# Context in two halves of tokens, the second one later, and the first norm's square root ahead of a values copy

## What is computed

```python
x = x + jnp.tanh(g_xattn[0]) * _L0_xattn_ref(_layernorm(x, axis=-1), ctx_4096, ctx_4096, pos, mask, Wq, Wk, Wv, Wo)
x = x + jnp.tanh(g_ffn[0]) * _L0_ffn_ref(_layernorm(x, axis=-1), W_q, scales, zeros, mask2, scale2, bias)
x = x + jnp.tanh(g_xattn[1]) * _L1_xattn_ref(_layernorm(x, axis=-1), ctx_4096, Wq1, bq, Wk1, bk)
x = x + jnp.tanh(g_ffn[1]) * _L1_ffn_ref(_layernorm(x, axis=-1), gate_w, expert_w, expert_b)

# in the first attention
q = (query @ Wq).reshape(nb, q_len, H, D).transpose(0, 2, 1, 3)
k = (key @ Wk).reshape(nb, q_len, KVH, D).transpose(0, 2, 1, 3)
v = (value @ Wv).reshape(nb, q_len, KVH, D).transpose(0, 2, 1, 3)
q = q * cos + _rotate_half(q) * sin
k = k * cos + _rotate_half(k) * sin
scores = jnp.where(mask == 0, -1e9, jnp.einsum("bhqd,bhkd->bhqk", q, k) / jnp.sqrt(D))
```

## Time and profile before

| what | us |
|---|---|
| median of 3 runs | 884.09 |
| lowest and highest run | 883.96 and 884.87 |
| the profiled execution's own time | 882.28 |
| its span, from the first to the last instruction | 880.5 |
| PE busy | 825.1 (94%) |
| DVE busy | 653.5 (74%) |
| POOL busy | 438.0 (50%) |
| ACT busy | 397.2 (45%) |

### The profile page before, as it was taken

One profiled execution on the slowest core, in us unless ns is written; L12 is line 12 of the kernel. 1 busy time (PEld: TensorE's weight loads), 2 busy tenths in 40 slices (PEclk: granted clock), 3 DMA queues, 4 the chain that ended last, 5 costly groups with the idle time before them and its releaser, 6 DMA issues. The chain is left out here.

```text
span 880.5 us, 13114 instructions
## 1 busy us (share of the span) xinstructions
PE 825.1 (94%) x4337; PEld 695.1 (79%) x4337; DVE 653.5 (74%) x1285; ACT 397.2 (45%) x1010; POOL 438.0 (50%) x386
## 2 busy tenths in 40 slices
PE   5889999999999999999999999999999999999980
PEld 4678888888888888888888888788778687778860
DVE  3888888867778876778876777856691658999965
ACT  4645245234334424324433433443314537879960
POOL 5489648436437634634833643530200148888840
PEclk9999999999999999999999999999999959999995
DMA  8401101101201100110220210100620677989517
GB/s 329 177 1 49 72 1 63 58 1 48 73 1 48 71 0 0 62 58 1 76 91 0 95 48 1 49 1 1 235 82 1 263 269 249 340 313 362 220 42 287
DMA packets 25945, 91.13 MB, mean 104 GB/s; under 512 B 6576, under 2 KB 7088, under 8 KB 18848
## 3 DMA queue, kind: packets, MB, share of 16 engines
q1 hardware_dynamic: 19744, 81.00, 25.1%
q0 software_dynamic: 6144, 9.46, 3.0%
HBM read 86.23 MB, written 14.68 MB: 115 GB/s over the span
## 5 line engine op out<-in xcount | busy, mean ns | idle before, releaser
L402 POOL TENSOR_TENSOR qT<-straight,turned 128x512 f32<-128x512 f32 x64 | 83.1, 1300 | 141.8 <-DVE turned L652 141.5
L518 ACT ACTIVATE probs<-bank,negmax 128x128 f32<-128x128 f32 x256 | 90.4, 365 | 130.8 <-DVE negmax L663 130.8
L652 DVE TENSOR_TENSOR turned<-bank,sinT 64x512 f32<-64x512 f32 x160 | 110.1, 688 | 2.2
L129 PE MATMUL bank<-xT_hi,wq_hi 128*128 128x512 f32 x256 | 104.2, 407 | 2.0 <-DVE xT_lo L105 2.0
L525 ACT ACTIVATE pT_hi<-bank 128x512 fp32r<-128x512 f32 x64 | 38.2, 598 | 139.0 <-PE bank L823 139.0
L131 PE MATMUL bank<-xT_hi,wq_lo 128*128 128x512 f32 x256 | 100.2, 392 | 0.0
L130 PE MATMUL bank<-xT_lo,wq_hi 128*128 128x512 f32 x256 | 100.0, 391 | 0.0
L131 PE MATMUL bank<-wo_hi,oT_lo 128*128 128x512 f32 x256 | 99.8, 390 | 0.0
L129 PE MATMUL bank<-wo_hi,oT_hi 128*128 128x512 f32 x256 | 99.7, 389 | 0.0
L130 PE MATMUL bank<-wo_lo,oT_hi 128*128 128x512 f32 x256 | 99.6, 389 | 0.0
L650 DVE TENSOR_TENSOR straight<-bank,cosT 128x512 f32<-128x512 f32 x80 | 55.3, 691 | 40.7 <-PE bank L131 36.9
(11 more groups left out here) (232 smaller groups left out, 2082.5 us busy)
## 6 DMA issues: line engine op xcount, KB each, us to landing
ring<-in_ew SPq DMA_DIRECT2D x28, 1024.0 KB, 8.8
raw_big<-in_wq SPq DMA_DIRECT2D x8, 1024.0 KB, 4.8
raw_big<-in_wo SPq DMA_DIRECT2D x8, 1024.0 KB, 4.8
early_w<-in_ew SPq DMA_DIRECT2D x8, 1024.0 KB, 10.0
ring<-picked SPq DMA_DIRECT2D x8, 512.0 KB, 7.6
raw_k<-in_wk SPq DMA_DIRECT2D x8, 256.0 KB, 5.1
ctx_raw<-in_ctxT SPq DMA_DIRECT2D x4, 512.0 KB, 6.1
raw_v<-in_wv SPq DMA_DIRECT2D x8, 256.0 KB, 5.0
```

The source lines that it names most:

```text
L129: nc.tensor.matmul(out_, hi, r_hi, start=start, stop=False)
L402: nc.gpsimd.tensor_tensor(dst, straight[:, k, :], turned[:, k, :], ALU.add).then_inc(rope_sum, 1)
L518: ex = nc.scalar.activation(probs[:, u % 2, h, :], bank_scores[u % 2][:, h * S:(h + 1) * S], ACT.Exp, bias=negmax[:, u % UNITS, h:h + 1], ...
L652: last = nc.vector.tensor_tensor(turned[dst, k, :], bank[src, :], sinT[src, tok], ALU.mult)
```

## The change

The context is fetched, copied and subtracted in two halves of tokens. The first half (tokens 0 to 511) keeps the four chunks and their places on SP, ACT and DVE, each now 128x512 in place of 128x1024. The second half is one transfer on SP behind the query weights, one ACT copy (128x2048) behind `queries_upper(0, 2)`, and one DVE subtraction (128x2048) behind `item_products(0, 2)`. It counts as the fifth step of `ctx_lo`, and PE, ACT and SP wait for five where they waited for four; on PE that wait is new and stands ahead of `make_values(0, 2)`. On ACT the square root of the first norm now stands ahead of the first values copy, with a square root of zeros before it. At the softmax of the second layer two semaphores, `g_max` and `g_nb`, became one, which counts both steps; the instructions are the same.

```diff
                     for c in range(KC):
-                        sp.dma_start(ctx_raw[:, c, :], a["ctxT"][:, c, :]).then_inc(in_ctx[c], 16)
+                        sp.dma_start(ctx_raw[:, c, 0:HALF], a["ctxT"][:, c, 0:HALF]).then_inc(in_ctx[c], 16)
...
                     sp.dma_start(raw_big[:, :], a["wq"][0].rearrange("p n -> p n")).then_inc(big_in, 16)
+                    sp.dma_start(ctx_raw[:, :, HALF:], a["ctxT"][:, :, HALF:]).then_inc(in_ctx_rest, 16)
                     sp.dma_start(mask_raw[:, :, :], a["mask"]).then_inc(in_mask, 16)
...
-                    sp.wait_ge(ctx_lo, KC)
+                    sp.wait_ge(ctx_lo, KC + 1)
                     sp.dma_start(wmask_raw[:, :, :], a["wmask"]).then_inc(f_words, 16)
...
                     for c in range(KC):
                         act.wait_ge(in_ctx[c], 16)
-                        nc.scalar.activation(cT_hi[:, c, :], ctx_raw[:, c, :], ACT.Copy).then_inc(ctx_hi, 1)
+                        nc.scalar.activation(cT_hi[:, c, 0:HALF], ctx_raw[:, c, 0:HALF], ACT.Copy).then_inc(ctx_hi, 1)
                     act.wait_ge(v_in, 32)
                     values_weight_upper(0, 0, raw_v)
                     values_weight_upper(1, 1, raw_v1)
+                    nc.scalar.activation(invtotal[:, 1, :], gates_raw[:, :], ACT.Sqrt, scale=0.0)
+                    norm_sqrt(act, 0, HALVES[0])
                     values_upper(0, 0)
-                    norm_sqrt(act, 0, HALVES[0])
                     values_upper(0, 1)
...
                     queries_upper(0, 2)
+                    act.wait_ge(in_ctx_rest, 16)
+                    nc.scalar.activation(cT_hi[:, :, HALF:], ctx_raw[:, :, HALF:], ACT.Copy).then_inc(ctx_hi, 1)
                     norm_upper(act, 0, 4)
...
-                    act.wait_ge(ctx_lo, KC)
+                    act.wait_ge(ctx_lo, KC + 1)
                     group(0, False)
...
                     for c in range(KC):
                         dve.wait_ge(ctx_hi, c + 1)
-                        nc.vector.tensor_tensor(cT_lo[:, c, :], ctx_raw[:, c, :], cT_hi[:, c, :].bitcast(F32),
+                        nc.vector.tensor_tensor(cT_lo[:, c, 0:HALF], ctx_raw[:, c, 0:HALF], cT_hi[:, c, 0:HALF].bitcast(F32),
                                                 ALU.subtract).then_inc(ctx_lo, 1)
...
                     item_products(0, 2)
+                    dve.wait_ge(ctx_hi, KC + 1)
+                    nc.vector.tensor_tensor(cT_lo[:, :, HALF:], ctx_raw[:, :, HALF:], cT_hi[:, :, HALF:].bitcast(F32),
+                                            ALU.subtract).then_inc(ctx_lo, 1)
                     norm_rest(dve, 0, 6)
...
                     turn_rotary(1)
+                    pe.wait_ge(ctx_lo, KC + 1)
                     make_values(0, 2)
```

More of the change, by code:

```diff
@@ L228, in program @@
             in_ctx = [sem(f"in_ctx{c}") for c in range(KC)]
+            in_ctx_rest = sem("in_ctx_rest")
             opening_step, rot_turned, rot_kept, ctx_hi, ctx_lo = (
@@ L1007, in program @@
         g_tables = sem("g_in_tables")
-        g_smm, g_max, g_nb, g_exp, g_inv, g_turned, g_pkept, g_omm, g_added = (
-            sem(f"g_{n}") for n in ("smm", "max", "nb", "exp", "inv", "turned", "pkept", "omm", "added"))
+        g_smm, g_nb, g_exp, g_inv, g_turned, g_pkept, g_omm, g_added = (
+            sem(f"g_{n}") for n in ("smm", "nb", "exp", "inv", "turned", "pkept", "omm", "added"))
         r_turned, r_kept, r_logits, r_best, r_onehot, r_coded, r_rank, r_place, r_at, r_codes = (
@@ L1247, in exps @@
                 def exps(n):
-                    act.wait_ge(g_nb, n + 1)
+                    act.wait_ge(g_nb, 2 * n + 2)
                     for b in range(4):
@@ L1426, in softmax_shift @@
                     dve.wait_ge(g_smm, n + 1)
-                    nc.vector.tensor_reduce(l1max[:, :], psum[4][:, :].rearrange("p (b k) -> p b k", b=4), AX.X, ALU.max).then_inc(g_max, 1)
-                    dve.wait_ge(g_max, n + 1)
+                    nc.vector.tensor_reduce(l1max[:, :], psum[4][:, :].rearrange("p (b k) -> p b k", b=4), AX.X, ALU.max).then_inc(g_nb, 1)
+                    dve.wait_ge(g_nb, 2 * n + 1)
                     nc.vector.tensor_scalar(l1nb[:, :], l1max[:, :], -SC1, None, ALU.mult).then_inc(g_nb, 1)
```

## The result

| | before | changed |
|---|---|---|
| median of 6 runs (lowest to highest) | 883.96 (882.70 to 884.87) | 890.88 (888.79 to 891.94) |
| ratio, 95% interval | | 1.0079 [1.0064, 1.0093] |
| profiled execution: time, span | 882.28, 880.5 | 891.94, 890.1 |

The change costs 6.9 us. A second set of runs gave 892.0 us against 883.61, a ratio of 1.010 [1.008, 1.012] or 8.4 us. The spans of the two profiled executions lie 9.6 us apart: the execution of before is 1.7 us under its median, that of after is the slowest of its six runs.

A forecast was written before the change was run, and what follows sets the result against it. PE, full from 51 us on, bounds the kernel, so the first scores' start decides: +6.3 (wait) and +2.2 (clock) make +8.5 us, against the median of 884.09 forecast as 892.6 us, range 889.0 to 895.0.

The forecast's parts named there:

- the clock holds: Rival: PE waits but its clock is not set back, or back at once; `wmask`'s chain decides, +6.6, 890.7 us; 14%.
- The wait on PE: Ahead of the values of sequences 4 and 5, PE waits 7.4 us for DVE's late subtraction; values start 6.3 us later.
- G: Opening up to ACT's first normalised tile: earlier x, `wv_lo` and root gain 2.0 us, between 0.75 and 2.7.
- The clock behind the gap: After PE's gap, products run at half rate for a dense stretch of 4.4 us, costing 2.2 us.
- The sum: Total delay: 6.3 for the wait plus 2.2 for the clock, +8.5 us.
- The second wait: SP's late `wmask_raw` delays POOL's sums: no scores before 57.4, +6.6 us, but hidden by about 1.9 us.
- the early gain did not arrive: Rival: the second half's subtraction ends before PE finishes its rotary transposes, so values start 1.1 us earlier, 883.0 us; 4%.
- The later part: Rival: a later part, where the clock stands at half before 727.8, gives back up to 8 us, about 885 us; 5%.
- get worse by 10 to 13 us: Rival: copies with row gaps cost more, or late `wmask` holds item 3 on POOL beside the cold clock: 896 us; 8%.

The follow-up runs named there:

- values and mask later: Changed kernel with PE's values of sequences 4 and 5 behind items 3 and 4, and POOL's first masked words behind item 4's sum: 884.63 us, 1.0023.
- 32 products: Changed kernel with 32 products without use for the output added on PE ahead of its wait for the second half: 889.6 us, 1.0075.
- the kernel with the values later: Changed kernel with PE's wait and values of sequences 4 and 5 behind items 3 and 4, POOL's mask work unmoved: 891.62 us, 1.0096.
- the kernel with the subtraction ahead: Changed kernel with DVE's subtraction of the second half ahead of item 2's products, not behind them: 883.48 us against 883.64, 1.0008.
- the first three of the versions tried last: From values and mask later: subtraction and `closed_key` ahead of item 2; also ACT's copy split; also 18 useless PE products: 887.97, 888.62, 887.73 us.
- the root alone: Kernel before with only the first norm's root, and a root of zeros before it, ahead of the first values copy: 883.14 us, 0.9999.

## Why the prediction was right, and where it was not exact

The time forecast, 892.6 us, stands 1.7 above the first median and 0.6 above the second, and both lie in the range. The first median lies beside the number of the rival "the clock holds", 890.7; the time alone would not tell the two apart, the traces do, since the clock did fall. The mechanism was right; that the sum came out so close is in part luck, as the terms show.

- **The wait on PE** came where forecast, with the releaser forecast: 6.36 and 7.20 us in the two traces (forecast 7.4). The copy took 1.90 (1.91), the subtraction 2.29 (2.3), and from the first normalised tile to the fourth query weights ACT took 36.24 - 29.90 = 6.34 (28.8 to 35.1, 6.3). The values started 7.35 and 6.58 later (6.3). Moving the subtraction alone gave the loss back, so the late subtraction is shown to be the cause.
- **G**, the early gain, was the term with the widest error. ACT's first normalised tile was forecast for 28.8; it came at 27.97 and 27.95 in two traces without early falls of the clock (values and mask later; 32 products), but at 29.90 and 29.38 in the changed kernel. G is 2.8 us at full clock, just over the upper bound of 2.7, and 0.9 to 1.4 with the falls (forecast 2.0). That the clock could fall in the opening I had not foreseen. Here lies the luck: in the trace with 32 products, without early falls, the values start 5.2 us later than before (42.99 against 37.80), and it took falls that the forecast did not have to bring that to 6.58 and 7.35.
- **The clock behind the gap**: values to scores took 15.20 and 14.77 us against 12.95, so 2.25 and 1.8 (forecast 2.2). This agrees with the Trainium skill, page "TensorE: Matmul & The Clock Gate", section "HAM oscillation — how this bites in real kernels", by which a gap in the stream sets the clock back: here the gap in the middle did it, as the tail's had. The half rate lasted 5.1 and 4.1 us from the start of the values (forecast 4.4). One of the two places from which I took those 4.4 is doubtful: the opening's products of 0.76 us stand in a stretch whose granted clock is 1.00 in the earlier trace rows, so that row alone doesn't show how long half rate lasts.
- **The sum**: 7.35 + 2.25 = 9.60 in the first trace, the whole distance of the two profiles, and 6.58 + 1.82 = 8.40 in the second (forecast 6.3 + 2.2 = 8.5). There it is the distance at the first scores; the spans are 10.2 apart, since 1.8 us more came behind them, most of it from the late fall of the clock.
- **The second wait**, `wmask`, was forecast hidden by 1.9 us. It was hidden in the changed kernel, by 1.04 us (POOL's wait for `turned` ahead of item 4's sum, as long as in the earlier trace rows), and decided as soon as the first was gone, which the kernel with the values later shows. It was issued at 45.12 (44.1) and landed 4.8 us later (5.4), at 49.9. What ACT's conversion behind it waited for was not this landing, as the forecast has it, but the values' copy ahead of it in ACT's order, which PE's late values held until 50.57.
- **The rivals**: the early gain did not arrive. The later part took nothing back: from the first scores on the two profiles are equal to the hundredth, by chance, and the second trace lost 1.8 us more there. It did not get worse by 10 to 13 us in either median.

## What to carry to other kernels

Splitting a load also splits its conversion, and every new piece takes a place in some engine's order: ask what that place waits for, not when the data lands. Here the second half was on the chip at 23.5 us, copied at 33.74, and subtracted only at 45.09, because its instruction stood behind one that waited for a different chain. When one such wait is taken away, look for the next one behind the same semaphore before timing it, and price a moved DVE instruction also by what POOL does beside it.

## What the runs showed of the hardware

**POOL's instructions take longer beside a DVE subtraction of two SBUF operands.** In eleven traces one POOL instruction of 128x512 ran beside the 2.28 to 2.29 us of the second half's `cT_lo`, and each took about 2.0 to 2.1 us longer than the 1.26 to 1.31 of the same instructions without such a neighbour, nearly the other's length. Four times it is `wq_lo`, 3.23 to 3.25 (the kernel with the subtraction ahead and the first three of the versions tried last), and seven times `qT`, 3.38 to 3.40, as in the changed kernel, where nothing on the path waited for it. The Trainium skill, page "SBUF — State Buffer", section "Who interferes with whom", says that a DVE instruction with two SBUF inputs contends with a GpSimd one that reads SBUF; these rows agree. That it takes two operands the runs do not show: beside `closed_key`, which reads one SBUF tile, POOL's sums took 1.73 to 1.80 us.

**The clock fell in the opening without a long stop.** The same program had one such fall in one trace (14.4 to 17.7 us) and two in another (16.1 to 19.5 and 29.8 to 33.2), and in the first stretch of the latter PE was at work all the while (3.00 of 3.00 us at 0.52). Ahead of the falls near 15 us, in seven traces, PE had waited 2.2 to 2.7 us for `wv_lo`; with 1.7 to 2.0 us the traces of three kernels show no fall there, and with 1.6 that of the root alone does. With products added in PE's gaps the traces show none before 44 us, one trace for each of the two kernels. What decides it the runs leave open. Where the values started at the same time, the fall near 15 us moved ACT's first normalised tile from 27.95 to between 29.23 and 29.46, by 1.3 to 1.5 us.
